# Layer-1 rows and the layer-1 edge sum in one stage of a graph kernel

## The chip, the cores and the metric

The kernel runs on one core of one Trainium2 chip. The metric is the device time of one execution in microseconds (us); lower is better. Engines are named as the profile names them: PE (TensorE matmul) and PEld (its weight loads), DVE (VectorE), ACT (ScalarE), POOL (GpSimd), SP (SyncE); SPq and ACTq are the queues on which SP and ACT issue DMAs.

## What is computed

Two layers over N = 6250 nodes with D = 256 features and E = 200000 edges, of which the second layer matters here:

```python
xn = _layernorm(x, axis=-1)
x = x + _L1_gnn_ref(xn, edge_weight, L1_gnn_W, L1_gnn_b, src, dst)
      + _L1_mix_ref(xn[None], L1_mix_Wq, ..., L1_mix_b2)[0]

def _L1_gnn_ref(x, edge_val, W, b, edge_row, edge_col):
    support = jnp.matmul(x, W)
    gathered = support[edge_col] * edge_val[:, None]
    return jax.ops.segment_sum(gathered, edge_row, num_segments=x.shape[0]) + b

def _L1_mix_ref(x, Wq, Wk, Wv, Wm, W1, W2, g1, b1, g2, b2):
    # Q, K = elu(x Wq)+1, elu(x Wk)+1; KV and sum K over all rows, per head
    msg = _layernorm((Q KV / (Q sum K)) @ Wm, g1, b1)
    h = relu(concatenate([x, msg]) @ W1) @ W2
    return x + _layernorm(h, g2, b2)
```

The first summand is the edge sum: for every edge a row of 256 values is fetched, scaled, and added into the row of another node. The second is row-wise work, once the sums over all rows exist.

## The kernel before

The rows of `x` live in SBUF as 50 blocks of 125 rows (`X[125, 50, 256]`), and row-wise work goes in 25 chunks (NC) of two blocks. Edges have been sorted by target block into records of three words (target, source, weight) in DRAM, and a group is 512 records (SUB = 4 times 128 partitions); there are NG = 391 groups. As a block's edges need not end with a group, the sum goes in NS = 440 steps, each one pair of (group, block). Tables in SBUF say for each step its group (`step_grp`) and block (`step_blk`), and for each group its first step (`first_step`).

**Stages.** `second_layer` does, in one block of straight-line code per engine, an FFN over the 25 chunks (L1148, L1158 on PE, L1484 on DVE), a pass over the chunks for K, V and the table `table1 = xn @ W` (L1189 on PE, L1318 to L1331 on ACT, L1512 on DVE), and then the **rows stage**: 27 turns (`for t in range(NC + 2)`, L1203 on), a software pipeline over chunks. Beside the first two, POOL moves the records into sorted order by indirect DMAs to DRAM (L557, batches of 17) as the positions become known. Then `end_phase()` closes the phase, and `edge_sums` runs as a phase of its own.

**One turn of the rows on PE** (in this order): the product with Wq (L1209), the turned rows of the last message and of `u` (L605), the product with W1 in four parts of which ACT takes pairs with a relu (L1234, ACT L1369), the message matmul (L1242, into two PSUM banks that DVE reads at L635 to L639), the turn of the next rows (L605), the product with Wm (L1255, into bank 6), and the product with W2 (L1264). DVE does the second half of Q (L1536), the last layer norm with its add to `X` (L578 to L592, L1542 to L1551), the division (L635 to L639), and the inner layer norm (L578 to L592, L1531).

**The edge sum.** `edge_walk` gives three parts. SP loads the records of a group (6 KB, L1797) into a ring of RING = 8 slots and, LAG = 4 groups later, waits for that group's gathers and counts `arrived`. POOL waits for the records, reads `first_step`, waits until the steps of the group eight before are `used` (L1820), and issues four indirect DMAs (L1824), each of 128 rows of 1 KB from `table1` into one slot of a ring that lies in `XN`. ACT loads the records of every step once more for DVE. For each step DVE makes the 0/weight matrix (L2142 and four times L2144, `weights`), PE multiplies it with the four gathered tiles into one of two banks (L2128, eight MATMUL records per step) and counts `used`, and DVE adds the bank to the block of `X` (L2156). PE and ACT run loops over 8 steps, DVE runs the first and last 8 steps in straight-line code and the rest in such a loop. Layer 0 has a walk of the same form (`edge_softmax`, loops too) over the same 391 groups and 440 steps, with more matmuls per step.

## Time and profile before

| | us |
|---|---|
| median of three runs | 9435.45 |
| the three runs | 9424.73 to 9456.72 |
| the profiled execution | 9495.87 |
| its span, first to last instruction | 9494.2 |
| PE / DVE / ACT / POOL busy | 5320.2 / 3713.0 / 1980.9 / 4700.6 |
| mean granted TensorE clock, of full speed | 0.763 |

No engine is busy all the time: stages follow each other, and each has a limit of its own. Read by stretches of the profiled execution: head and layer-0 rows up to about 1594, the layer-0 edge walk to about 4340, FFN and K/V of layer 1 to about 6212, the rows stage from there to 6674, the layer-1 edge sum to 9033, and the end (norm, experts, output). POOL's DMA instructions are counted busy while they issue; "idle before" tells how long the engine stood before an instruction and what ended that, where "issue" and "remote" are times in which the profile shows no releaser.

### The profile page before, as it was taken

To read this page: it belongs to the slowest core of one execution; us is meant where nothing else is said; L and a number is where in the kernel's file an instruction comes from. 1 tells how busy PE (TensorE), PEld (TensorE's weight loads), DVE (VectorE), ACT (ScalarE), POOL (GpSimd) and SP (SyncE) were. 2 spreads that over 40 slices of the span, in tenths; PEclk is the share of its full clock that TensorE was granted. 3 is DMA by queue.
4 is the path that set the end of the run, shared out by engine and by line. 5 is a ranking of instruction groups with operands and counts; after the bars stand their busy time and mean duration, and the time that the engine had idled before them with its cause. 6 is when DMAs were issued, how large, how long until landed. Compare 5 with 4: busy or idle time off the path is not lost. (4 is left out here: it accounts for less than half of the span.)

```text
span 9494.2 us, 116847 instructions
## 1 busy us (share of the span) xinstructions
PE 5320.2 (56%) x22050; PEld 3899.7 (41%) x22051; DVE 3713.0 (39%) x14367; ACT 1980.9 (21%) x4706; POOL 4700.6 (50%) x5589
## 2 busy tenths in 40 slices
PE   0431276777877778886053461089444544454469
PEld 0320154455555555554043350078333333333357
DVE  6340154444444444556142240046333333333355
ACT  6110043333333333333021120033000000000034
POOL 3476501555555555554725326600566666666600
PEclk9765577888888888887576685599677777777789
DMA  2100001333333333332000000000233333333300
GB/s 76 30 4 3 5 1 27 86 84 85 84 84 80 78 80 79 81 79 73 3 1 3 2 19 5 5 7 1 76 89 90 89 90 90 91 90 89 89 21 18
DMA packets 505060, 495.26 MB, mean 52 GB/s; under 512 B 374732, under 2 KB 401877, under 8 KB 504149
## 3 DMA queue, kind: packets, MB, share of 16 engines
q0 software_dynamic: 200192, 432.72, 16.7%
q1 hardware_dynamic: 154712, 33.52, 2.0%
q10 hardware_dynamic: 150013, 27.32, 1.7%
q8 instruction: 65, 1.06, 0.0%
q14 instruction: 78, 0.64, 0.0%
HBM read 462.90 MB, written 30.23 MB: 52 GB/s over the span
## 5 line engine op out<-in xcount | busy, mean ns | idle before, releaser
L1824 POOL DMA_INDIRECT XN<-table,XN x3128 | 2988.6, 955 | 993.3 <-issue 935.8
L557 POOL DMA_INDIRECT records<-slot_rec,slot_pos x1564 | 1535.6, 982 | 594.1 <-issue 594.1
L2128 PE MATMUL gcn_psE<-XN,gcn_pE 128*125 x3520 | 1130.5, 485 | 1227.8 <-DVE gcn_pE L2144 905.5
L75 POOL TENSOR_TENSOR cell<-cell 1x1 int32<-1x1 int32 x874 | 162.1, 186 | 2727.2 <-DMA XN<-records 972.7
L2128 PEld LDWEIGHTS gcn_psE<-XN,gcn_pE 128*125 128x125 f32 x3520 | 829.7, 245 | 1528.6 <-issue 1367.3
L1953 PE MATMUL gat_psE<-XN,gat_pE 128*125 x3520 | 1066.1, 455 | 252.7 <-issue 173.1
L1953 PEld LDWEIGHTS gat_psE<-XN,gat_pE 128*125 128x125 f32 x3520 | 751.7, 225 | 399.3 <-issue 275.8
L2156 DVE TENSOR_TENSOR X<-X,gcn_psE 125x256 f32 x440 | 184.4, 419 | 1560.1 <-remote 1113.7
L1937 PE MATMUL gat_psS<-XN,gat_kTs 25*125 25x512 f32 x880 | 586.8, 750 | 152.1 <-ACT XN L1982 113.6
L2144 DVE TENSOR_SCALAR gcn_pE<-iota_n,gcn_lk,gcn_rec 128x125 f32<-128x125 f32 x1760 | 500.7, 364 | 16.0
L1573 ACT ACT_TABLE_LOAD x1 | 1.3, 1283 | 2364.9 <-PEq L117 2364.9
L1944 PE MATMUL gat_psP<-ident,XN 125*128 125x125 f32 x1760 | 309.8, 305 | 198.9 <-ACT gat_sc L2002 148.1
L2032 DVE TENSOR_SCALAR gat_pen<-gat_psB,iota_p 125x512 f32<-125x512 bf16 x440 | 328.7, 747 | 199.6 <-remote 185.0
L2006 ACT ACTIVATE gat_pE<-gat_psP 128x500 f32<-128x500 f32 x440 | 256.9, 584 | 683.4 <-PE gat_psP L1944 349.2
L1944 PEld LDWEIGHTS gat_psP<-ident,XN 125*128 125x128 f32 x1760 | 248.0, 161 | 289.8 <-ACT gat_sc L2002 170.2
L1926 PEld LDWEIGHTS gat_psA<-ident,XN 128*25 128x25 f32 x1760 | 162.6, 113 | 447.8 <-issue 399.2
L1926 PE MATMUL gat_psA<-ident,XN 128*25 128x128 f32 x1760 | 316.4, 310 | 29.2 <-ACT XN L1991 24.3
L1158 PE MATMUL b_bank<-room,b_wf 128*128 128x250 f32 x800 | 193.5, 396 | 246.6 <-issue 161.4
L2043 DVE COPY gat_mo<-edge_m 125x1 f32 x440 | 67.8, 154 | 658.7 <-PE gat_psS L1937 278.1
L1189 PE MATMUL b_bank<-b_wkv,room 128*125 128x256 f32 x400 | 108.9, 433 | 385.3 <-issue 382.1
L745 PE MATMUL a_bank<-room 128*125 128x256 f32 x200 | 74.3, 535 | 432.8 <-ACT room L866 290.1
L2001 ACT ACTIVATE XN<-XN,gat_nm 125x512 f32<-125x512 f32 x440 | 310.9, 707 | 10.2 <-issue 10.2
(448 smaller groups left out, 8516.5 us busy)
## 6 DMA issues: line engine op xcount, KB each, us to landing
XN<-table,XN POOLq DMA_INDIRECT x3128
records<-slot_rec,slot_pos POOLq DMA_INDIRECT x1564
XN<-records SPq DMA_DIRECT2D x782, 6.0 KB
gat_rec<-records ACTq DMA_DIRECT2D x440, 6.0 KB
gcn_rec<-records ACTq DMA_DIRECT2D x440, 6.0 KB
table<-XN ACTq DMA_DIRECT2D x5, 1250.0 KB
table<-room ACTq DMA_DIRECT2D x25, 250.0 KB
out_x<-X SPq DMA_DIRECT2D x25, 250.0 KB
```

Of the source, the lines that this page charges most:

```text
L557: pool.indirect_dma_start(out=rec_d[1], out_offset=bass.IndirectOffsetOnAxis(ap=slot_pos[:, h, j:j + 1], axis=0), in_=slot_rec[:, h, j, :] ...
L1158: last = pe.matmul(psH[i % 2][:, 0:TOK], wf1[:, j, i * P:(i + 1) * P], xT[:, j, :], start=(j == 0), stop=(j == KF - 1))
L1824: pool.indirect_dma_start(out=rows_t[:, s, j, :], out_offset=None, in_=table, in_offset=bass.IndirectOffsetOnAxis(ap=rec_g[:, s, j, 1:2].b ...
L1926: pe.transpose(psA[0:SMALL, j * P:(j + 1) * P], q_rows[:, s % 2, j * SMALL:(j + 1) * SMALL], ident[:, :])
L1937: pe.matmul(psS[d][0:B, :], kTs[:, d, :], qT[:, d, :], start=True, stop=True).then_inc(s_mm, 1)
L1944: last = pe.transpose(psP[:, j * B:(j + 1) * B], pT[:, d, j * P:(j + 1) * P], ident[0:B, 0:B])
L1953: last = pe.matmul(psE[d][0:B, 0:D], pE[:, d, j * B:(j + 1) * B], rows_t[:, slot_of(g), j, 0:D].rearrange("p a w -> p (a w)"), start=(j == ...
L2001: act.activation(pT[:, d, :], S[:, d, :], ACT.Exp, bias=nm[:, d:d + 1], scale=SC, accum_out=rs[:, d:d + 1])
L2006: act.activation(pE[:, d, :], psP[:, 0:SUB * B], ACT.Copy).then_inc(p_done, 1)
L2032: dve.tensor_scalar(pen[:, d, :], psB[0:B, :], iota_p[0:B, 0:1], -BIG, ALU.not_equal, ALU.mult).then_inc(pen_done, 1)
L2128: last = pe.matmul(psE[d][0:B, 0:D], pE[:, d, j, :], rows_t[:, slot_of(g), j, :].rearrange("p a w -> p (a w)"), start=(j == 0), stop=(j == ...
L2144: last = dve.tensor_scalar(pE[:, d, j, :], iota_n[:, :], lk[:, d, j:j + 1], rec_t[:, s, j, 2:3], ALU.is_equal, ALU.mult)
```

## The change

The phase `edge_sums` is gone; its steps are done inside the rows stage of `second_layer`, and what is left of them in a loop at that stage's end.

- **ROWS_ALONE = 12.** Turns 0 to 11 have no steps. In each of the turns 12 to 26 there are four bursts of BURST = 2 steps: 15 x 8 = 120 steps. The other 320 follow in a loop of two steps per iteration.
- **Gathers.** POOL begins them when `rows_free` is set, before turn 0, in a ring `b_ring` of its own (8 slots of 4 KB per partition), since `XN` still holds rows. POOL now waits only for a group's records. It is SP that waits for `used` of the group eight before, and then loads the records into a ring in which DVE also reads them. ACT issues no record loads any more.
- **PSUM.** The steps take banks 6 and 7. Wm's product goes to bank 2 and W1's to banks 4 and 3, which the message matmul also uses, so PE has new waits: the message matmul for ACT's second relu pair (`r_done`) and for `m_done`, Wm's product for DVE's division (`u_done`).
- **Memory and loads.** The FFN's and K/V's weights lie in `b_ring` and are overwritten by the gathers; the other five weights lie in `room` and are loaded after `freed`, beside `src`.
- DVE solves the inner layer norm in the turn of its moments, not at the start of the next.

The core of the diff, in the order SP, POOL, PE (a step, then places of a turn, then the loop), DVE (a burst):

```diff
+ROWS_ALONE = 12
...
+                        def body(t, s):
+                            if not (isinstance(t, int) and t == 0):
+                                n = sp.value_load(first_step[1][0:1, bass.ds((t - 1) * RING + s + 1, 1)], min_val=1, max_val=NS)
+                                sp.wait_ge(used, n)
+                            sp.dma_start(rec_g[:, s, :, :].rearrange("p s w -> p (s w)"),
+                                         rec_v[bass.ds(t * RING + s, 1), :, :].rearrange("g p w -> (g p) w")).then_inc(records[s], 16)
+                            if near(t, s, -LAG):
+                                arrive(*near(t, s, -LAG))
...
                         mv.pool(pool)
+                        pool.wait_ge(mv.settled, 2 * turns)
...
+                        pool.wait_ge(rows_free, 1)
+
+                        def body(t, s):
+                            pool.wait_ge(records[s], t * 16 + 16)
+                            settle(pool, cell[0:1, 0:1], settled, t * RING + s)
+                            for j in range(SUB):
+                                pool.indirect_dma_start(out=ring[:, s, j, :], out_offset=None, in_=table1,
+                                                        in_offset=bass.IndirectOffsetOnAxis(ap=rec_g[:, s, j, 1:2].bitcast(I32), axis=0)).then_inc(got[s], 16)
...
+                        def edge_sum(x, d):
+                            g = group_of(pe, x)
+                            pe.wait_ge(weighed, x + 1)
+                            if not (isinstance(x, int) and x < 2):
+                                pe.wait_ge(added, x - 1)
+                            for j in range(SUB):
+                                last = pe.matmul(psE[d][0:B, 0:D], pE[:, d, j, :],
+                                                 ring[:, bass.ds(g % RING, 1), j, :].rearrange("p a w -> p (a w)"),
+                                                 start=(j == 0), stop=(j == SUB - 1))
+                            last.then_inc(used, 1)
...
+                                    if pair:
+                                        pe.wait_ge(u_done, min(t, NC))
...
+                                if t >= ROWS_ALONE:
+                                    burst()
                             if t < NC:
                                 pe.wait_ge(q_done, t + 1)
                                 pe.wait_ge(u_done, t)
+                                if t >= 2:
+                                    pe.wait_ge(m_done, t - 1)
+                                    pe.wait_ge(r_done, 2 * (t - 2) + 2)
...
                                 pe.wait_ge(m_done, k)
+                                if t < NC:
+                                    pe.wait_ge(u_done, t + 1)
...
+                        with loop(pe, (NS - early_steps) // BURST) as t:
+                            for d in range(BURST):
+                                edge_sum(t * BURST + (early_steps + d), d)
...
+                        def burst():
+                            nonlocal summed
+                            for d in range(BURST):
+                                add_sum(summed + d, d)
+                            summed += BURST
+                            for d in range(BURST):
+                                weights(summed + d, d)
...
-        def edge_sums():
```

In a turn from 12 on, PE's bursts stand behind the first and the second pair of W1, behind the turned next rows and behind Wm's product; DVE's stand behind the second half of Q, behind the last norm with its add, behind the division, and behind the inner norm.

On PE, in one turn of the rows stage before (L1234 is W1's product, the turn begins with L1209):

```order
L1209 MATMUL b_bank<-room 128x250 x4
L605 MATMUL b_bank<-ident,room 128x125 x8
L1234 MATMUL b_bank<-room 128x250 x16
L1242 MATMUL b_bank<-b_kvd,room 125x132 x4
L605 MATMUL b_bank<-ident,XN 128x125 x4
L1255 MATMUL b_bank<-b_wm,room 125x256 x4
L1264 MATMUL b_bank<-b_wm,room 125x256 x8
```

And in the changed kernel in a turn from 12 on, from the turned rows (L606) over the first pair of W1 (L1338) into the first step of the first burst (L1151 reads the group, L1288 is the step's product):

```order
L606 MATMUL b_bank<-ident,room 128x125 x8
L1338 MATMUL b_bank<-room 128x250 x8
L1151 TENSOR_LOAD step_grp
L1151 ISA x2
L1288 ISA
L1288 MATMUL b_bank<-b_ring,room 125x256
L1288 ISA
L1288 MATMUL b_bank<-b_ring,room 125x256
L1288 ISA
L1288 MATMUL b_bank<-b_ring,room 125x256
L1288 ISA
L1288 MATMUL b_bank<-b_ring,room 125x256
```

W1's sixteen matmuls are split into two pairs of eight, and a burst of two steps stands behind each pair, behind the turned next rows, and behind Wm's product.

On POOL, in the loop of the edge sum before, the wait for `used` (with the load of `first_step`) stands ahead of the four gathers of a group:

```order
L1820 ISA
L1820 TENSOR_LOAD first_step
L1820 ISA x2
L74 REGISTER_ALU
L75 TENSOR_TENSOR cell<-cell 1x1
L1824 DMA XN<-table,XN 128x256 x4
```

In the changed kernel that load and its wait stand on SP, ahead of the load of the records for which POOL waits (`room` is where the records now go):

```order
L1181 TENSOR_LOAD first_step
L1181 ISA x2
L1183 DMA room<-records 128x12
L1181 TENSOR_LOAD first_step
L1181 ISA x2
L1183 DMA room<-records 128x12
```

So a group's slot is freed to SP and reaches POOL only by way of the record load.

## Rows read from the trace of the kernel before

**Rows 1.** PE over one turn of the rows stage: start us, us, line, operation, idle before

```profile
6404.02 6.93 PE L1234 MATMUL b_bank<-room 128*128 128x250 f32 x32
6410.79 1.06 PE L1242 MATMUL b_bank<-b_kvd,room 128*125 128x132 f32 x8
...
6412.12 1.89 PE L1255 MATMUL b_bank<-b_wm,room 128*125 128x256 f32 x8
...
6417.30 1.85 PE L1209 MATMUL b_bank<-room 128*128 128x250 f32 x8
...
6421.05 0.62 PE L605 MATMUL b_bank<-ident,room 125*128 125x125 f32 x4 [1.47 <-ACT room L1356]
6421.50 6.93 PE L1234 MATMUL b_bank<-room 128*128 128x250 f32 x32
```

**Rows 2.** ACT in the same turn: the relu of W1's second pair

```profile
6410.99 0.83 ACT L1369 ACTIVATE room<-b_bank,b_bias 128x250 f32<-128x250 f32 x2 [2.55 <-PE b_bank L1234]
```

**Rows 3.** DVE in the same turn: second half of Q, last add, division

```profile
6403.04 0.68 DVE L1536 SCALAR_TENSOR_TENSOR room<-b_bank,room 128x500 f32<-128x500 f32 x1 [2.76 <-ACT room L1352]
...
6409.51 0.69 DVE L1551 TENSOR_TENSOR X<-X,room 125x512 f32<-125x512 f32 x1
...
6412.45 0.76 DVE L639 TENSOR_TENSOR room<-b_bank,b_z 125x256 f32<-125x256 f32 x2
```

**Rows 4.** Busy us (x instructions) of PE, PEld, DVE, ACT, POOL; clock; DMA share; GB/s

```profile
2300.00:2900.00 600.00, 474.58 (x2032) 313.30 (x2032) 291.88 (x1302) 219.90 (x649) 339.77 (x426) 0.83 0.33 84
5610.00:6170.00 560.00, 70.48 (x251) 55.56 (x249) 4.84 (x7) 19.70 (x34) 392.34 (x428) 0.55 0.04 6
6415.00:6674.00 259.00, 234.82 (x1216) 206.55 (x1214) 160.29 (x661) 78.51 (x157) 0.00 (x0) 1.00 0.00 1
7300.00:7900.00 600.00, 288.99 (x911) 212.46 (x912) 194.25 (x681) 0.00 (x0) 402.72 (x502) 0.73 0.33 90
```

**Rows 5.** Start of the edge sum on POOL, its last add on DVE

```profile
6686.47 0.18 POOL L75 TENSOR_TENSOR cell<-cell 1x1 int32<-1x1 int32 x1 [513.22 <-DMA XN<-records]
...
9032.44 0.42 DVE L2156 TENSOR_TENSOR X<-X,gcn_psE 125x256 f32 x1 [1.31 <-PE gcn_psE L2128]
```

**Rows 6.** Groups by line, 6660 to 9050: xcount, busy us, mean ns, idle before

```profile
L1824 POOL DMA_INDIRECT XN<-table,XN x1564 | 1498.1, 958 | 463.6 <-issue 422.1 <-remote 2.1 <-PE gcn_psE L2128 1.8
...
L2144 DVE TENSOR_SCALAR gcn_pE<-iota_n,gcn_lk,gcn_rec 128x125 f32<-128x125 f32 x1760 | 500.7, 364 | 16.0
L2156 DVE TENSOR_TENSOR X<-X,gcn_psE 125x256 f32 x440 | 184.4, 419 | 1560.1 <-remote 1113.7 <-issue 318.2 <-PE gcn_psE L2128 127.0
```

**Rows 7.** A cycle of the edge sum: POOL, then DVE

```profile
7516.91 0.95 POOL L1824 DMA_INDIRECT XN<-table,XN  x1 [0.30 <-issue]
7520.76 0.18 POOL L75 TENSOR_TENSOR cell<-cell 1x1 int32<-1x1 int32 x1 [2.90 <-remote]
...
7520.63 0.42 DVE L2156 TENSOR_TENSOR X<-X,gcn_psE 125x256 f32 x1 [12.46 <-remote]
...
7544.78 0.42 DVE L2156 TENSOR_TENSOR X<-X,gcn_psE 125x256 f32 x1 [11.13 <-remote]
```

**Rows 8.** PE at the end of the edge sum, POOL done

```profile
9020.10 3.71 PE L2128 MATMUL gcn_psE<-XN,gcn_pE 128*125 x16 [0.53 <-DVE gcn_pE L2144]
```

**Rows 9.** FFN chunks on DVE, two ahead of and two during POOL's moves

```profile
4933.06 0.69 DVE L1484 TENSOR_TENSOR room<-b_bank,b_bf 125x512 f32<-125x512 f32 x1 [2.59 <-PE b_bank L1148]
4947.14 0.69 DVE L1484 TENSOR_TENSOR room<-b_bank,b_bf 125x512 f32<-125x512 f32 x1 [2.69 <-PE b_bank L1148]
...
5167.83 0.69 DVE L1484 TENSOR_TENSOR room<-b_bank,b_bf 125x512 f32<-125x512 f32 x1 [112.31 <-remote]
5358.93 0.69 DVE L1484 TENSOR_TENSOR room<-b_bank,b_bf 125x512 f32<-125x512 f32 x1 [171.53 <-remote]
```

**Rows 10.** DMA queues, 5600 to 6180: packets, MB, share of 16 engines

```profile
q8 instruction: 2, 0.03, 0.0%
```

**Rows 11.** DMA issues of the whole page: count, KB each, median us to landing

```profile
slot_rec<-spill_rec SPq DMA_DIRECT2D x92, 25.5 KB, 1.7
```

**Rows 12.** POOL's gathers in 6700 to 9000: min/median/max ns

```profile
L1824 POOL DMA_INDIRECT XN<-table,XN x1541: 943/949/1072, 6699.5 to 8999.2; - x193
```

More of the change, by code:

```diff
@@ L1248, in _ @@
                                 turn_rows(pe, psT, xn_rows, t + 1).then_inc(turned, 1)
+                            if t >= ROWS_ALONE:
+                                burst()
                             if 1 <= t <= NC:
@@ L1257, in _ @@
                                 last.then_inc(g_mm, 1)
+                            if t >= ROWS_ALONE:
+                                burst()
                             if t >= 2:
@@ new lines, in weights @@
+                        def weights(x, d):
+                            g = group_of(dve, x)
+                            rec = rec_g[:, bass.ds(g % RING, 1), :, :].rearrange("p a s w -> p (a s) w")
+                            dve.wait_ge(arrived, g + 1)
+                            if not (isinstance(x, int) and x < 2):
+                                dve.wait_ge(used, x - 1)
+                            steps(dve.tensor_scalar(lk[:, d, :], rec[:, :, 0], step_node[1][:, bass.ds(x, 1)], None, ALU.subtract))
+                            for j in range(SUB):
+                                last = dve.tensor_scalar(pE[:, d, j, :], iota_n[:, :], lk[:, d, j:j + 1], rec[:, j, 2:3], ALU.is_equal, ALU.mult)
+                            last.then_inc(weighed, 1)
@@ new lines, in add_sum @@
+                        def add_sum(x, d):
+                            b = dve.value_load(step_blk[1][0:1, bass.ds(x, 1)], min_val=0, max_val=NB - 1)
+                            ub = one(X[:, bass.ds(b, 1), :])
+                            dve.wait_ge(used, x + 1)
+                            if not (isinstance(x, int) and x < 1):
+                                dve.wait_ge(added, x)
+                            dve.tensor_tensor(ub, ub, psE[d][0:B, 0:D], ALU.add).then_inc(added, 1)
+                        summed = 0
```

223 lines of the change are left out of this document (120 added, 103 removed).

## Prediction

> **What bounds the kernel now.** I read three views, in this order: the table of busy time by stretch, to see which engine each stage leans on; then the timelines of one turn of the rows and of one cycle of the edge sum; then the waits at the edge sum's start and end.
>
> The rows stage is PE's. PE is busy 234.82 of 259 us at full clock and POOL does nothing at all [rows 4]; a turn takes 6421.50 - 6404.02 = 17.48 us, in which PE idles only 1.47 us, waiting for ACT [rows 1]. Turn 12 begins with Q's product at 6417.3 [rows 1].
>
> The edge sum belongs to POOL and to something that POOL's stream does to the others. It runs from 6686.47 to 9032.86 [rows 5]. A gather costs POOL 0.958 us and 0.27 us (422.1 / 1564) of issue [rows 6], so with the settling instruction (0.18 [rows 5]) a group can't go below about 5.1 us; in 600 us POOL does 502 / 5 = 100.4 groups, 5.98 us each, and PE 911 / 8 = 113.9 steps, 5.27 us each [rows 4]. Neither figure is what PE and DVE need: with POOL done, two steps take 3.71 + 0.53 = 4.24 us, 2.12 us each [rows 8]. The cycle shows where the rest goes. POOL issues without a break up to 7517.86, stands 2.90 us, goes on at 7520.76. DVE had stood 12.46 us and goes on at the same moment, 7520.63, then works until 7544.78 - 11.13 = 7533.65 and stands again [rows 7]. So PE and DVE get about **13 us of free running** after each pause of POOL, and next to nothing until the next pause. That this is POOL's stream and not the edge sum's own chain is seen in the FFN, where nobody waits for POOL: a chunk takes 4947.14 - 4933.06 = 14.08 us, but beside POOL's moves, which never pause, 5358.93 - 5167.83 = 191 us [rows 9]; in the K/V pass beside the moves PE is busy 70 of 560 us [rows 4]. I don't know the mechanism; I use the two lengths.
>
> **The change, part by part.** The stretch that changes runs from 6417.3 (turn 12) to 9032.9, 2615.6 us, plus turns 0 to 11.
>
> *Turns 0 to 11, new waits on PE.* The message matmul now waits for ACT's second relu pair: that ends at 6410.99 + 0.83 = 6411.82 [rows 2], while the matmul began at 6410.79 [rows 1]: +1.1 us. Wm's product waits for DVE's division, which ends at 6413.21, 1.4 us after the message matmul's 6411.85 [rows 1, 3], where it used to begin 0.3 us after it: +1.1 us. The 1.47 us wait for ACT hangs on the work behind Wm's product, so it stays. Ten turns of 2.2 us: **+22**.
>
> *Turns 0 to 2, POOL fills its ring.* Eight groups are 41 us of stream without a pause; the free running covers 13, so 28 us are starved. These turns wait for latency anyway; I take **+25** (between 5 and 35).
>
> *Turns 12 to 26.* A turn has 8 steps = 7.1 groups, 36 us of POOL's time at 5.1. PE has 234.82 / 14.8 turns = 15.9 us of rows and 8 times 1.9 to 2.0 us of steps [rows 4, 8], 32 us. DVE has 160.29 / 14.8 = 10.8 and 8 times 500.7 / 440 + 0.42 = 1.56, 23 us [rows 4, 6]. They don't run side by side, though. PE's third burst needs the weights of DVE's second burst, and that stands behind the last norm: from 6403.04 to 6410.20, 7.2 us [rows 3]. Walking through one turn with bursts of 4.0 us on PE and 3.8 us on DVE, PE waits some 6 us there, 3 us ahead of the fourth burst, and 1.5 us for ACT as now: about **42 us of free running a turn**. Some turns' worth of it falls in starved time. Steps free slots, and POOL fills them in one go: 15.3 us free (13 and the 2.3 of the next paragraph) free 2.6 groups, 13 us of stream, then a pause of 2.9 + 2.3; 18.4 us in all for 15.3 of work, a turn of 50 us. Without the 2.3, it is 45.5. The layer-0 walk is the nearest whole case: 2032 matmuls at 22 a step are 92 steps of 6.49 us, with PE busy 5.14 us in each [rows 4], a factor of 1.26; on PE's own 32 us and one wait of 6 that gives 48. I take **49 us**, and keep 42 (7.1 groups at POOL's present 5.98) and 60 as ends. Ring full at turn 12: -10. Together 15 x 49 - 10 = **725**.
>
> *The loop of 320 steps.* DVE and PE do per step what they did. What changes is a slot's way: `used` reached POOL directly, now it reaches SP, which issues the record load, whose landing POOL awaits. The nearest load lands in 1.7 us [rows 11]; with SP's own part 2.3 us more at each pause. PE and DVE run free in it, so it isn't lost: 13 us now carry 24.15 / 5.27 = 4.6 steps, 2.84 us each, so 15.3 us are 5.4 steps, 4.8 groups, 24.4 + 5.2 = 29.6 us, 5.5 a step. ACT's 440 small loads go, which can only help. I take **5.45** (5.27 if the latency costs nothing, 5.8 if it adds fully to each group cycle): 320 x 5.45 = **1744**.
>
> Nothing for the loads of weights after `freed`: their first use is behind the FFN, and POOL, not they, sets the K/V pass. What lies between the rows' end, near 6674, and the first gather at 6686.47 [rows 5] is in the 2615.6 and has no successor.
>
> *Sum:* 22 + 25 + 725 + 1744 = 2516 against 2615.6: **-100 us**. The sum is made against the profiled execution (9495.87, span 9494.2), 0.64% above the median of 9435.45; taken off in proportion it is 99, and gives **9336**.
>
> *A rule against the change.* DVE's weights last 1.14 us a step and now also meet the norms [rows 6]; POOL's gathers take 943/949/1072 ns in all the edge sum [rows 12], so what DVE does beside them costs at most 0.12 us. The Trainium skill, "SBUF — State Buffer", section "Who interferes with whom", says that DVE's `tensor_scalar` in a two-port mode and GpSimd exclude each other for the whole instruction. By that rule 8 x 1.14 = 9 us would be added to a turn's POOL time. The rows don't bear it out.
>
> **Rivals.**
>
> *A. POOL alone sets the pace.* 42 us a turn, 5.27 a step, start-up 10: 22 + 10 + 620 + 1686 = 2338, -277: **9160**. For it: in the cycle PE and DVE need 2.12 of 5.27 us, and POOL paused 15% of the time. Against: the layer-0 walk, whose PE need per group is like a turn's, has POOL at 600 / 85.2 = 7.0 us a group [rows 4].
>
> *B. The steps merely add.* A turn costs its 17.5 and 8 x 5.3 = 60 us, as if the rows only ran where POOL stands: 47 + 15 x 60 - 10 + 1700 = 2637, +21; with 5.27 in the loop and no start-up loss 2598, -18. Between them: **9435**, no change that can be told (I take 0.3%, 28 us, as what a measurement tells).
>
> *C. Slower: the rows starve.* The rows' chain crosses PE, ACT and DVE a dozen times a turn, the edge sum's three times a step. If POOL, whose records are loaded ahead, streams four groups and more in a row as now, a cycle of 24 us has 13 free, and 42 us of turn take 42 x 24.15 / 13 = 78 us; half-way to that, 64: 47 + 950 + 1744 = 2741, +125: **9560**. It decides from 56 us a turn on. For it: the 14-fold FFN chunk in straight-line code [rows 9]. Against: POOL can't stream what isn't freed, and a turn frees a group only each 6 us. One doubt about it can be put aside: if straight-line code starved because its instructions couldn't be fetched, turns would suffer and loops not; but in the 580 us of the crawling K/V pass one such queue moved 2 blocks [rows 10]. The Trainium skill, "Runtime: NRT & Kernel Launch", section "Instruction fetch mechanics", has fetch in blocks of 256 instructions over a DMA queue of its own, mostly hidden; this row agrees.
>
> *D. The record load is the new bound.* With SP starved like the others, a slot takes 5 us and more to reach POOL; 5.8 a step and 52 a turn: 47 + 770 + 1856 = 2673, +57: **9492**.
>
> *E. POOL locked out by DVE* (the rule above as a mechanism): 9 us a turn over 15 turns, +135 on the forecast: **9471**.
>
> **How the numbers follow.** Forecast (turn 46 to 53, -160 to -35): 0.42. A and what lies towards it: 0.23. B: 0.12. C: 0.14. D: 0.07. E: 0.02. Likeliest: 9336. The range must hold 8 in 10: down it takes in A with its 9160, up D and the near side of C: **9160 to 9510**. Faster by over 0.3%: the forecast and A, 0.65. Within 0.3%: B, 0.12. Slower by over 0.3%: C, D, E, 0.23.
>
> **What would show it.** Turns 2 to 11 at 19.7 us from one W1 product to the next, with PE waiting for ACT ahead of the message matmul and for DVE ahead of Wm's. POOL issuing 32 gathers from before turn 0 and then standing until turn 12. Turns from 12 at 46 to 53 us (42: A; 60: B; above 56: C); in the loop 5.3 to 5.6 us a step, with pauses of POOL of some 5 us ended by a record load where they were 2.9. The forecast is wrong if a turn's free-running need isn't near 42 us, or if POOL's short pauses between single groups already let the others run (then A), or don't (then C).

## The result: slower by 1.2%, where 1.1% faster was forecast

| | before | after |
|---|---|---|
| median, us | 9432.50 (4 runs) | 9551.83 (4 runs) |
| lowest to highest | 9424.73 to 9456.72 | 9536.08 to 9578.22 |
| profiled execution, its span | 9495.87, 9494.2 | 9536.08, 9534.4 |
| ratio after / before, 95% interval | | 1.0124, 1.0108 to 1.0139 |

The forecast was 9336 with a range of 9160 to 9510; the time is 216 us above the one and 42 above the other. The two profiled executions differ by only 40 us, since that of before is 63 us above its median and that of after 16 us below. On which chip the first ran isn't on record. A later profile of the same kernel, called before2 below, took 9431.92 us (span 9430.2), and I compare after with that one. Its first message matmul of the rows begins at 6175.5, that of after at 6181.8; what lies behind the last add is 461.4 and 463.6 us. Nearly all of the 104 us between the two spans is in the middle: 2793.3 us in before2, 2889.0 in after.

### The profile after

PE in the turns that have no steps (start, us, engine, line, operation, idle before and what ended it):

```profile
6254.84 1.14 PE L1350 MATMUL b_bank<-b_kvd,room 128*125 128x132 f32 x8 [1.01 <-ACT room L1487]
6257.53 1.96 PE L1367 MATMUL b_bank<-room 128*125 128x256 f32 x8 [1.13 <-DVE room L640]
6274.93 1.14 PE L1350 MATMUL b_bank<-b_kvd,room 128*125 128x132 f32 x8 [1.01 <-ACT room L1487]
```

The two new waits are where the prediction put them, and a turn takes 6274.93 - 6254.84 = 20.09 us where it took 17.48 [rows 1].

A turn with eight steps, in parts: POOL's first operation of a group (L76; its gathers, which follow, are left out), PE, ACT and DVE, from four timelines of the same turn.

```profile
6732.52 0.18 POOL L76 TENSOR_TENSOR cell<-cell 1x1 int32<-1x1 int32 x1 [3.03 <-DMA room<-records]
...
6739.21 0.18 POOL L76 TENSOR_TENSOR cell<-cell 1x1 int32<-1x1 int32 x1 [1.26 <-DMA room<-records]
...
6744.72 0.22 POOL L76 TENSOR_TENSOR cell<-cell 1x1 int32<-1x1 int32 x1
...
6748.97 1.85 PE L1310 MATMUL b_bank<-room 128*128 128x250 f32 x8
...
6749.82 0.19 POOL L76 TENSOR_TENSOR cell<-cell 1x1 int32<-1x1 int32 x1
...
6754.89 0.18 POOL L76 TENSOR_TENSOR cell<-cell 1x1 int32<-1x1 int32 x1
6755.67 0.23 DVE L1651 TENSOR_SCALAR room<-room,step_node 128x4 f32 x1 [4.45 <-issue]
...
6762.71 0.59 ACT L1468 ACTIVATE room<-b_bank 128x500 f32<-128x500 f32 x1 [14.60 <-DMA X<-in_x]
...
6764.56 1.07 PE L606 MATMUL b_bank<-ident,room 125*128 125x125 f32 x4 [13.31 <-ACT room L1474]
...
6773.75 0.18 POOL L76 TENSOR_TENSOR cell<-cell 1x1 int32<-1x1 int32 x1 [13.81 <-DMA room<-records]
```

From 6739.21 POOL streams four groups without a pause. PE's product with Wq, which ACT needs, is over at 6750.82 by the profile (the ends of matmuls are modelled), but ACT starts on it at 6762.71, when the stream is over (the DMA named there was long done). PE stands 13.31 us, and then it is POOL that waits for 13.81 us, since nobody had freed a slot. Over the last eleven pitches (from the start of one message matmul to the start of the next) a turn takes 55.5 us.

The trace also has the times of the semaphore updates, and they say what was late. The update that tells ACT of the product is recorded at 6762.69, 11.87 us behind the product's end, and ACT starts 0.02 us later. In the turns without steps from turn 2 on it comes 0.01 us behind the end. In ten of the twelve turns 13 to 24 it comes 4.7 to 13.0 us behind it, each time 1.9 to 3.0 us after the end of POOL's last gather. So ACT was ready, and it is PE's signal (or the true end of the matmul, which the profile doesn't show) that came late. PE's waits for ACT at this place in the turns with steps (us in total, times, longest):

```profile
PE b_bank L606 <- ACT room L1474: 123.4, 13, 14.5
```

That is 9.5 us a turn where it was 1.47 [rows 1].

The loop. Busy us by stretch of the last 320 steps (PE, PEld, DVE, ACT, POOL, clock, DMA share, GB/s), first of before2, then of after:

```profile
7314.00:8969.00 1655.00, 814.24 (x2553) 599.24 (x2551) 545.06 (x1910) 0.00 (x0) 1109.45 (x1384) 0.73 0.33 90
```

```profile
7266.00:9070.00 1804.00, 806.92 (x2542) 578.97 (x2543) 583.63 (x1908) 0.00 (x0) 1102.00 (x1374) 0.73 0.29 81
```

PE's and POOL's work is the same; the stretch takes 149 us longer. Where they went is seen in what POOL's settling operation, the first of each group, waited for in these stretches (us in total, times, longest). Before2:

```profile
POOL cell L75 <- remote: 173.4, 69, 3.3
POOL cell L75 <- PE gcn_psE L2128: 12.7, 11, 2.4
POOL cell L75 <- issue: 8.7, 16, 0.8
```

After:

```profile
POOL cell L76 <- DMA room<-records: 333.8, 92, 11.9
POOL cell L76 <- issue: 17.1, 15, 2.2
```

That is 194.8 against 350.9 us. The loop is POOL's stream plus POOL's pauses. Between the starts of the first and the last of the 320 adds it is 1654.5 - 194.8 = 1460 us in before2, 1805.3 - 350.9 = 1454 in after. This sum is used in all that follows. It came out at 1440 to 1470 us for every kernel on such chips with whole gathers and the settling operation unchanged, whatever was done to the steps.

### The profile page after: what moved, and what is told of

It reads as the page before. It is cut to its first block and busy times, and to the rows that moved or that the text cites. A ratio compares the mean times of both kernels' runs of the same rounds, so it can differ in the third digit from the quotient of the medians.

```text
span 9534.4 us, 117269 instructions
## 1 busy us (share of the span) xinstructions
PE 5231.6 (55%) x22050; PEld 3839.0 (40%) x22051; DVE 3769.7 (40%) x14367; ACT 1979.1 (21%) x4706; POOL 4696.8 (49%) x5590
## 5 line engine op out<-in xcount | busy, mean ns | idle before, releaser
L1992 POOL DMA_INDIRECT XN<-table,XN x1564 | 1486.5, 950 | 528.3 <-issue 511.9
L1205 POOL DMA_INDIRECT b_ring<-table,room x1564 | 1497.5, 957 | 469.8 <-issue 432.2
L1288 PE MATMUL b_bank<-b_ring,room 128*125 x3520 | 1071.6, 463 | 1181.7 <-DVE room L1653 803.6
L76 POOL TENSOR_TENSOR cell<-cell 1x1 int32<-1x1 int32 x874 | 166.4, 190 | 2749.4 <-DMA room<-records 810.6
L1288 PEld LDWEIGHTS b_bank<-b_ring,room 128*125 128x125 f32 x3520 | 782.7, 231 | 1462.3 <-issue 1324.0
L2121 PE MATMUL gat_psE<-XN,gat_pE 128*125 x3520 | 1040.9, 446 | 253.1 <-issue 175.2
L1653 DVE TENSOR_SCALAR room<-iota_n,room 128x125 f32<-128x125 f32 x1760 | 515.0, 355 | 272.3 <-issue 195.8
L1662 DVE TENSOR_TENSOR X<-X,b_bank 125x256 f32 x440 | 185.4, 421 | 742.1 <-issue 339.9
L1651 DVE TENSOR_SCALAR room<-room,step_node 128x4 f32 x440 | 107.1, 243 | 595.4 <-issue 449.9
L1240 PE MATMUL b_bank<-room,b_ring 128*128 128x250 f32 x800 | 192.4, 396 | 242.3 <-issue 236.8
L1271 PE MATMUL b_bank<-b_ring,room 128*125 128x256 f32 x400 | 111.9, 442 | 374.7 <-issue 369.9
```

The source lines that it names most:

```text
L1205: pool.indirect_dma_start(out=ring[:, s, j, :], out_offset=None, in_=table1, in_offset=bass.IndirectOffsetOnAxis(ap=rec_g[:, s, j, 1:2].bi ...
L1288: last = pe.matmul(psE[d][0:B, 0:D], pE[:, d, j, :], ring[:, bass.ds(g % RING, 1), j, :].rearrange("p a w -> p (a w)"), start=(j == 0), st ...
L1653: last = dve.tensor_scalar(pE[:, d, j, :], iota_n[:, :], lk[:, d, j:j + 1], rec[:, j, 2:3], ALU.is_equal, ALU.mult)
L1992: pool.indirect_dma_start(out=rows_t[:, s, j, :], out_offset=None, in_=table, in_offset=bass.IndirectOffsetOnAxis(ap=rec_g[:, s, j, 1:2].b ...
L2121: last = pe.matmul(psE[d][0:B, 0:D], pE[:, d, j * B:(j + 1) * B], rows_t[:, slot_of(g), j, 0:D].rearrange("p a w -> p (a w)"), start=(j == ...
```

## The experiments

Two theories on the loop, each from a line of the change, and one on the turns:

- **F**, VectorE's step got longer. It is three things in one: a register load of the group, register addresses for the records, and the wait for the group's gathers (`arrived`), which TensorE had before. With POOL done, an add, its 0.68 us gap and the weights take 2.98 us a step where they took 2.12 [rows 8]:

```profile
9057.11 0.42 DVE L1662 TENSOR_TENSOR X<-X,b_bank 125x256 f32 x1 [0.57 <-issue]
...
9059.92 0.42 DVE L1662 TENSOR_TENSOR X<-X,b_bank 125x256 f32 x1 [0.21 <-issue]
9061.02 0.23 DVE L1651 TENSOR_SCALAR room<-room,step_node 128x4 f32 x1 [0.68 <-issue]
9061.40 1.11 DVE L1653 TENSOR_SCALAR room<-iota_n,room 128x125 f32<-128x125 f32 x4
9063.08 0.42 DVE L1662 TENSOR_TENSOR X<-X,b_bank 125x256 f32 x1 [0.57 <-issue]
```

Two steps take 9063.08 - 9057.11 = 5.97 us.

- **D**, the record load stands between a freed slot and POOL (rival D of the prediction).
- **C**, in the turns the rows starve beside POOL's stream (rival C).

A group of runs shares one chip, and each ratio is against before on that chip. "Turn" is the mean of the last eleven pitches; "loop" is us a step over the last 320 steps (from the first to the last of their adds, divided by 319); "waits" is what POOL's settling operation waited there, in us. A chip "starves" where the other engines nearly stop beside POOL's stream, as in rows 9.

| kernel | chip's before | ratio (95%) | turn | loop | waits |
|---|---|---|---|---|---|
| before2 | 9436.6 | one run | 17.5 | 5.19 | 195 |
| after | 9432.5 | 1.0124 (1.0108 to 1.0139) | 55.5 | 5.66 | 351 |
| f_before | 9434.5 | 1.0224 (1.0182 to 1.0265) | 17.5 | 5.62 | 326 |
| d_before | 9434.5 | 1.0101 (1.0081 to 1.0121) | 17.5 | 5.43 | 289 |
| own_records | 9434.5 | 1.0092 (1.0063 to 1.0121) | 58.3 | 5.38 | 275 |
| pool_waits | 9434.5 | 0.9994 (0.9982 to 1.0007) | 53.5 | 5.40 | 266 |
| hoist_after | 9514.7 | 1.0132 (1.0111 to 1.0152) | 56.1 | 5.82 | 395 |
| hoist_pool | 9514.7 | 0.9969 (0.9959 to 0.9978) | 51.3 | 5.48 | 294 |
| both_undone | 9514.7 | 0.9934 (0.9918 to 0.9951) | 54.8 | 5.23 | 215 |
| alone_26 | 9514.7 | 1.0284 (1.0267 to 1.0301) | 20.1 | 5.67 | 339 |
| pace_d | 9505.6 | 1.0025 (1.0010 to 1.0041) | 54.4 | 5.54 | 218 |
| early_own2 | 9505.6 | 0.9869 (0.9840 to 0.9898) | 54.6 | | |
| quarter | 6736.3 | one run | 42.6 | 2.98 | |
| pace_a | 6736.3 | 1.0326 (1.0309 to 1.0343) | | 4.85 | |
| pace_b | 6736.3 | 1.1072 (1.1054 to 1.1091) | | 6.13 | |
| after2 | 6723.5 | 1.0085 (1.0068 to 1.0102) | 42.6 | 4.44 | 1 |
| pace_c | 6723.5 | 1.0323 (1.0306 to 1.0341) | 44.6 | 4.86 | |
| early_pool | 6723.5 | 1.0118 (1.0101 to 1.0135) | 41.0 | | |
| early_own | 6723.5 | 1.0378 (1.0361 to 1.0395) | 47.8 | | |

### f_before and d_before: each suspect alone, in the kernel before

f_before gives VectorE the form of a step that it has in the changed kernel (the records lie in 16 slots, addressed by the group, and ScalarE loads them there). The wait for `arrived` goes from PE to DVE with it:

```diff
 def weights(t, s):
     x, d = t * RING + s, s % 2
+    g = group_of(dve, x)
+    rec = rec_t[:, bass.ds(g % 2 * RING + s, 1), :, :].rearrange("p a s w -> p (a s) w")
+    dve.wait_ge(arrived, g + 1)
     dve.wait_ge(rec_ready[s], t * 16 + 16)
```

d_before moves the wait for `used`:

```diff
 # SyncE
+    if which and not (isinstance(t, int) and t == 0):
+        n = sp.value_load(first_step[which][...])
+        sp.wait_ge(used, n)
     load_records(sp, t * RING + s, rec_g[:, s, :, :], group_ready[s])
```

> The kernel before, with only VectorE's part of a step written as in the changed kernel: the group is read from its table into a register, the wait for the gathers stands on VectorE, and the five reads of the records go by a register. GpSimd and SyncE are untouched. Theory F (VectorE's step got longer: 2.98 us instead of 2.12 with GpSimd done, so fewer steps fit into a cycle of free running): slower, by 0.1 to 0.4 us a step, 9480 to 9600 against 9433. Theory D (the record load in a slot's way back to GpSimd): no change, within 20 us of 9433.

> The kernel before, with only the wait for `used` of the second walk moved from GpSimd to SyncE, ahead of the record load. VectorE's step is untouched. Theory D: each of the 80 odd pauses of GpSimd gets about 1 to 2.3 us longer and ends in a record load, 5.45 to 5.8 us a step in place of 5.23: 9510 to 9680. Theory F: within 30 us of 9433.

Measured: 9636.39 and 9533.85 us against 9434.54, so +202 and +99. Both theories hold, and each alone is dear; F's price is above the 47 to 167 us that were expected. The two don't add up: the loops lose 0.43 and 0.24 us a step, the changed kernel with both loses 0.47. POOL's waits in the last 320 steps tell how. F:

```profile
POOL cell L75 <- PE gcn_psE L2131: 243.1, 67, 9.8
POOL cell L75 <- remote: 74.8, 42, 2.9
```

D:

```profile
POOL cell L75 <- DMA XN<-records: 274.0, 67, 5.4
POOL cell L75 <- issue: 15.3, 11, 2.2
```

Counting pauses of over 1 us in that stretch: before2 has 75 of 2.46 us on average, F 96 of 3.24, D 70 of 3.99, and after, with both, 90 of 3.73. In the changed kernel with only F left (pool_waits, below) it is 99 of 2.56, with only D left (own_records) 68 of 3.86. **F makes more pauses, D makes each longer**; in f_before they also got longer. With F fewer steps, so fewer freed slots, fit between two pauses (3.3 in place of 4.3), and that is what I had left out.

No run takes the three parts of F from each other. What the moved wait ended is on record, though:

```profile
DVE gcn_lk L2148 <- SPq L1804: 41.0, 16, 6.7
```

In before2 PE waited 3.5 us for the same count in these 320 steps. The moved wait is a part of F, then, and the instructions need not be all of the rest. What F adds with POOL done is seen at this kernel's end, where each step has a gap that before does not have:

```profile
9162.14 0.42 DVE L2162 TENSOR_TENSOR X<-X,gcn_psE 125x256 f32 x1
9163.18 0.23 DVE L2148 TENSOR_SCALAR gcn_lk<-gcn_rec,step_node 128x4 f32 x1 [0.62 <-issue]
9163.55 1.11 DVE L2150 TENSOR_SCALAR gcn_pE<-iota_n,gcn_lk,gcn_rec 128x125 f32<-128x125 f32 x4
9164.79 0.42 DVE L2162 TENSOR_TENSOR X<-X,gcn_psE 125x256 f32 x1
```

A step is 9164.79 - 9162.14 = 2.65 us here, 0.53 more than the 2.12 of before. Over 440 steps the 202 us are 0.46 each, so F costs about what it adds to a step with POOL done. In that gap stand one register load, 0.31 us by the trace, and five short instructions that the profile doesn't count as busy either. The Trainium skill, "Runtime: NRT & Kernel Launch", section "Instruction fetch mechanics", gives about 200 ns for a register load. The trace has half as much again for the load alone.

### own_records and pool_waits: each suspect taken out of the changed kernel

own_records: ScalarE loads the records of every step once more, 8 at a time in a turn, into 16 slots with fixed addresses; VectorE reads those.

```diff
+    if t >= ROWS_ALONE:                       # ScalarE, in a turn
+        first = 8 * (t - ROWS_ALONE)
+        for x in range(first + 8 if first else 0, first + 16):
+            step_records(x, x)
...
 def weights(x, d, ...):                       # VectorE
-    g = group_of(dve, x)
-    rec = rec_g[:, bass.ds(g % RING, 1), :, :]...
-    dve.wait_ge(arrived, g + 1)
+    rec = rec_t[:, base % SLOTS, :, :]
+    dve.wait_ge(rec_ready[base % SLOTS], ...)
```

pool_waits: 16 record slots, SyncE loads ahead, POOL waits for `used` as before the change.

```diff
 # SyncE
-    sp.wait_ge(used, n)
-    sp.dma_start(rec_g[:, s, ...], ...)
+    sp.dma_start(rec_g[:, h * RING + s, ...], ...)
 # POOL
     pool.wait_ge(records[h * RING + s], ...)
+    n = pool.value_load(first_step[1][...])
+    pool.wait_ge(used, n)
```

> The changed kernel, with VectorE's records loaded once more for each step by ScalarE into a ring of 16 slots with fixed addresses (the wait for the gathers is TensorE's again, the loop of VectorE has 16 steps an iteration). SyncE's wait and record load stay. Theory F: VectorE's step back to 2.1 us free; 5.35 us a step in the loop instead of 5.66 and turns of 50 us instead of 55.4: about 9370. Theory D: within 40 us of 9552. Theory C (the rows starve in the turns, whatever a step costs): the loop gains, about 100 us, the turns stay at 54 us or more: about 9450.

> The changed kernel, with the wait for `used` on GpSimd as before the change, and the records of a group loaded ahead by SyncE into a ring of 16 slots. VectorE's step stays as long as it is. Theory D: pauses go from 3.7 us back to 2.7, some 100 us in the loop and the like share in the turns: 9400 to 9450. Theory F: less than 60 us, 9500 to 9550. Theory C: turns stay at 54 us or more in either case.

Measured: 9515.92 and 9428.12. In the loop both give back what was expected (5.66 to 5.38 and to 5.40; waits 351 to 275 and to 266), the one as much as the other, though F had been twice as dear as D in the kernel before. In the turns they part: pool_waits brings 55.5 down to 53.5, own_records takes it up to 58.3, so that its total misses F's 9370 and C's 9450 and lies where D alone would have put it. The turns rise most likely because ScalarE's eight loads stand in the middle of the rows' chain (early_own and early_pool, below, differ in the same way; no run isolates the loads). So theory C survives in both: with either suspect out, a turn stays above 53 us.

pool_waits equals before within its interval: the overlap gains what F and the starved turns cost.

### hoist_after, hoist_pool, both_undone, alone_26

The hoist moves VectorE's load of the group ahead of the wait for `used`, where four weight instructions are still in work:

```diff
 def add_sum(x, d, ahead=False):
     b = dve.value_load(step_blk[1][0:1, bass.ds(x, 1)], ...)
+    g = group_of(dve, x + BURST) if ahead else None
     dve.wait_ge(used, x + 1)
```

> The changed kernel, with one instruction moved on VectorE: a step's register load of its group stands ahead of the wait for `used`, beside that of the block, where four weight instructions of the step before are still in work. Theory F by exposure (what hurts is that the load of 0.68 us stands behind the wait): nearly all that VectorE's form cost comes back, 5.4 us a step in the loop instead of 5.66, 9552 - 90 or more: 9400 to 9470. Theory F by count (each instruction costs in starved time, wherever it stands): under 30 us, 9520 to 9560.

> The same with the wait for `used` on GpSimd and the records loaded ahead into 16 slots. Theories F (exposure) and D together: 5.2 us a step in the loop, turns of 50: 9428 - 70 to - 110, so 9320 to 9360, under both kernels. F by count: 9400 to 9430.

> The changed kernel with VectorE's records loaded by ScalarE for each step and the wait for `used` on GpSimd, so both parts of a step as before the change: the loop has to run at the 5.2 to 5.25 us of before (F and D are all that there is), 320 x 0.42 = 135 less than 9552. The turns: 58 us as in the kernel with ScalarE's loads alone if it is these loads that hold up the rows, 50 if it was not. 9400 with the first, 9300 with the second.

> The changed kernel with ROWS_ALONE = 26: 8 steps in the last turn, 432 in the loop. If a turn of 55.4 us is one of 20.1 plus 8 steps of 4.4 us, the overlap gives 1.25 us for each of the 112 steps moved, and undoing it costs 140: 9690. Theory C (the rows starve so much that a step in a turn costs what it does in the loop): 9552 within 30.

hoist_after: ratio 1.0132, no better than the 1.0124 of after, with 395 us of waits in the loop. **Theory F by exposure fell**: it matters little on which side of the wait the load stands. Its end, with POOL done, shows why the hoist could bring nothing:

```profile
9165.48 0.42 DVE L1663 TENSOR_TENSOR X<-X,b_bank 125x256 f32 x1 [0.92 <-issue]
9165.88 0.23 DVE L1651 TENSOR_SCALAR room<-room,step_node 128x4 f32 x1
...
9168.65 0.42 DVE L1663 TENSOR_TENSOR X<-X,b_bank 125x256 f32 x1 [1.28 <-issue]
...
9171.45 0.42 DVE L1663 TENSOR_TENSOR X<-X,b_bank 125x256 f32 x1 [0.92 <-issue]
```

The gap behind the add is gone, and the gap ahead of it has grown from 0.21 and 0.57 us to 0.92 and 1.28. Two steps take 9171.45 - 9165.48 = 5.97 us, what they took in after. The load was moved, not hidden. So these runs speak for F by the length or the number of the instructions, which they can't tell apart. hoist_pool gained 0.25% on pool_waits (0.9969 against 0.9994, on two chips), in its turns (51.3 us), not in its loop.

both_undone: the loop is back at 5.23 us a step and its waits at 215 us, so F and D together are all of the loop's loss. At 0.9934 it is faster than both kernels, though its turns of 54.8 us lie between the 58 and the 50 that were expected.

alone_26 is the same code with the overlap undone. It cost 1.0284 / 1.0124, 1.6% or 150 us, with 140 expected: a step in a turn does cost (55.5 - 20.1) / 8 = 4.4 us, one in the loop 5.7. **The overlap works**; it is bought with a dearer step and a dearer slot.

### quarter: what a turn needs

One of a group's four gathers is issued, on top of pool_waits; it leaves out the other three, so three quarters of the gathered rows are stale:

```diff
-    for j in range(SUB):
+    for j in range(SUB if isinstance(t, int) and t == 0 else 1):
         pool.indirect_dma_start(out=ring[:, s, j, :], ...)
```

> The kernel with the wait for `used` on GpSimd and 16 record slots, in which GpSimd fetches only one of a group's four tiles (the first eight groups are fetched whole), so three quarters of the gathered data are stale: a group costs GpSimd 1.5 us and its stream is never long. It shows what a turn and a step need when nobody is starved. Theory C (in a turn, what lies above the forecast's 42 us of free running is starvation by GpSimd's stream): turns of 40 to 44 us, steps of 3.0 us in the loop, 8450 to 8550. Rival (the turn's chain is simply longer than it was walked through): turns of 50 us and more, 8600 and up.

Message matmuls of two turns in a row, and VectorE's adds of the loop:

```profile
4742.29 1.06 PE L1365 MATMUL b_bank<-b_kvd,room 128*125 128x132 f32 x8
4784.73 1.06 PE L1365 MATMUL b_bank<-b_kvd,room 128*125 128x132 f32 x8
```

```profile
5835.91 0.42 DVE L1677 TENSOR_TENSOR X<-X,b_bank 125x256 f32 x1 [0.57 <-issue]
...
5841.88 0.42 DVE L1677 TENSOR_TENSOR X<-X,b_bank 125x256 f32 x1 [0.58 <-issue]
```

42.44 us a turn (42.6 over eleven) and 2.98 us a step. The walk had said 42. This run came onto a chip where POOL's stream starves nobody (next section), and there the changed kernel with all its gathers (after2) takes 42.6 us a turn too. So it is the pair after and after2, one kernel on two chips, that gives the price: 55.5 - 42.6 = 12.9 us a turn beside POOL's stream. Of these, 8 are in the wait shown above. On after2 the same wait is

```profile
PE b_bank L606 <- ACT room L1474: 18.3, 13, 1.5
```

and PE's update for ACT comes 0.01 us behind the product's end in every turn. The granted clock was lower in the turns of after as well, 0.81 against 0.89, but PE's busy time there is 508 against 485 us for the 15 turns, which is 1.5 us a turn. The rest is then C's, not the rows' own chain.

### after2, pace_a, pace_b, pace_c, early_pool, early_own: chips that don't starve

The chip of quarter ran before in 6736 us, and another one in 6723, where the others need 9430 to 9520. The kernels are the same. What differs is the thing that I had taken for a property of the kernel. FFN chunks beside POOL's moves, on after2:

```profile
3271.50 0.69 DVE L1602 TENSOR_TENSOR room<-b_bank,b_bf 125x512 f32<-125x512 f32 x1 [2.31 <-PE b_bank L1230]
3285.58 0.69 DVE L1602 TENSOR_TENSOR room<-b_bank,b_bf 125x512 f32<-125x512 f32 x1 [2.53 <-PE b_bank L1230]
```

14.08 us, where before took 191 beside the same moves [rows 9]. On these two chips POOL's stream starves nobody, and every stage with such a stream is short.

> The changed kernel unchanged. On a chip that starves: ratio 1.012 again. On a chip without starvation: a turn is 42.5 us or a little more, its 7.1 groups taking 36 us of GpSimd; a step in the loop is bound by GpSimd, 5.07 x 391 / 440 = 4.5 us, before and after alike; per step moved a turn saves 4.5 - (42.5 - 20.1) / 8 = 1.7 us, 120 of them 204, less 2.6 x 12 = 31 for the new waits: ratio 0.975.

After2 shows the expected turn (42.6 us) and loop (4.44 us a step, POOL alone; it waits 0.8 us in 320 steps), and yet the ratio is 1.0085, not 0.975. One row points at the reason. PE, the first step of turn 12:

```profile
4251.61 3.77 PE L1288 MATMUL b_bank<-b_ring,room 128*125 x8 [322.53 <-DVE room L1653]
```

PE stood 322.53 us. Turn 0 begins near 3700 us here, and 27 turns of 17.5 us would end near 4172, ahead of POOL's moves (4238 us). So the kernel before has its whole rows stage beside the moves, where it costs nothing. The changed kernel keeps 15 turns back to mix them with steps, and steps can't begin before the records are in place. It then pays in POOL's time: 58.0 us of waits for records in the turns,

```profile
POOL cell L76 <- DMA room<-records: 58.0, 18, 6.5
```

which matches the 57 us of the result (6780.27 - 6723.47). That before hides all 27 turns there is worked out from these rows and not shown; before2, meant to show it, came onto a chip that starves. The time that its expectation works out for such a chip, 6712 us, is 11 us under the 6723 measured on the chip of after2.

> The kernel before, unchanged. On a chip without starvation (near 6730): the K/V pass and all 27 turns of the rows end before GpSimd's moves do, near 4240, so the rows cost nothing there, and the edge sum takes 440 x 4.5 = 1980 us bound by GpSimd; 4240 + 30 + 1980 + 462 = 6712. Rival: some turns stand behind the moves, 17.5 us each, and the edge sum is quicker than GpSimd's 5.07 us a group allow, which can't be. On a chip that starves: turn 0 near 6180 to 6250, pauses of GpSimd of about 200 us in the last 320 steps, 9430 to 9520.

It showed there what the section on the result uses: 9431.92 us, turn 0 near 6175, 195 us of waits.

On the other kernels these chips say little of starvation, and the expectations for it came to nothing:

> The same kernel, whole, with GpSimd's tiny settling operation ahead of each group's gathers made larger (125x256 in place of 1x1, an estimated 0.3 to 0.6 us a group). Theory P (short gaps in GpSimd's stream feed the others as well as its long pauses do): cycles vanish, turns go from 54 to 47 or less, the loop to 5.1 to 5.3 us a step; 9428 - 100 to - 150. Rival (only a real standstill frees them, any work on GpSimd just adds): 391 groups of 0.4 us, some + 100: 9530.

> The same with three such operations in a row, an estimated 1 to 1.8 us a group. Theory P: no starvation is left, the turn is the larger of 42 us and 7.1 groups of 6.5 us = 46, the loop 5.8 us a step by GpSimd alone: 9400 to 9450. Rival: + 400 us or more.

> The kernel with the wait for `used` on GpSimd and 16 record slots, with the settling operation of 125x256 (0.62 us instead of 0.18) ahead of each group's gathers; the same kernel as pace_a, to be seen on a chip on which GpSimd's stream starves the others (before near 9430 to 9520). There theory P (short gaps feed the others): turns of 47 us or less, ratio to before 0.97 to 0.985. Rival (a gap of half a us feeds nobody): 391 x 0.45 = 175 us more, ratio 1.01 to 1.02. On a chip without starvation (before near 6736) it repeats 1.033.

> The kernel with the wait for `used` on GpSimd, 16 record slots and the group's register load ahead of the wait, with ROWS_ALONE = 2: 80 more steps in turns. A step in a turn costs 4.0 to 4.2 us, one in the loop 5.4: 80 x 1.2 = 96 us less than with 12: ratio to before 0.985 to 0.99 on a chip that starves. Theory C (early turns starve more, since GpSimd starts with an empty ring): 0.995 or more.

> The kernel with both parts of a step as before the change (ScalarE's record loads for VectorE, `used` on GpSimd), with ROWS_ALONE = 2. 80 steps move from 5.2 to 4.2 us: ratio 0.985 on a chip that starves, in place of 0.9934 with 12.

The larger settling operation took 0.62 us, as in this row of pace_d,

```profile
7704.37 0.63 POOL L1220 TENSOR_TENSOR b_wr<-b_wr 125x256 f32<-125x256 f32 x1
```

and where POOL is the only bound, work on it merely adds: pace_a and pace_c lie 3.3 and 3.2% above before, pace_b, with three of them, 10.7%. early_pool shows turns of 41.0 us and early_own of 47.8, the difference being, most likely, ScalarE's eight loads a turn; with more turns held back from under the moves both are slower than after2.

### pace_d and early_own2: the same two on a chip that starves

pace_d, on top of pool_waits:

```diff
-    settle(pool, cell[0:1, 0:1], settled, t * RING + s)
+    for i in range(1):
+        pool.wait_ge(settled, (t * RING + s) * 1 + i)
+        pool.tensor_tensor(wr[:, :], wr[:, :], wr[:, :], ALU.subtract).then_inc(settled, 1)
```

early_own2 is both_undone with ROWS_ALONE = 2.

> The same kernel as pace_a and pace_c, once more for a chip that starves. Theory P (short gaps feed the others): turns of 47 us or less, ratio to before 0.97 to 0.985. Rival (a gap of half a us feeds nobody): 391 x 0.45 = 175 us more than the 9428 of its base, ratio 1.01 to 1.02. On a chip without starvation it repeats 1.032.

> The same kernel as early_own, once more for a chip that starves: 80 steps more in turns, each 1.0 us cheaper there than in the loop: ratio 0.985, in place of 0.9934 with ROWS_ALONE = 12. Rival: ScalarE's 8 loads a turn hold up the rows as in early_own (47.7 us a turn instead of 42.5 without starvation), and starvation comes on top: turns of 58 and more, ratio 1.00.

pace_d: 1.0025, between the two theories. POOL's operations got 391 x 0.44 = 172 us longer, the kernel only about 30 (0.9994 to 1.0025). In the loop the stream took 92 us more by the sum of the first section (1768 - 218 = 1550 against 1723 - 266 = 1457), and the waits fell by 48; the turns stayed at 54.4. So a gap of half a us doesn't pay for itself. Whether it feeds the others a little, or the waits are only shorter because POOL comes to them later, isn't told apart.

early_own2: 9391.24 against 9505.62, **ratio 0.9869**, as expected. It beats before here, and after by its ratio of 1.0124: 80 more steps went into turns of 54.6 us, and the second layer's steps have their short form. On a chip that doesn't starve the same kernel is 3.8% slower than before (early_own). Which of the two is better is a question of the chip, not of the code.

## Why the prediction was wrong, by its own steps

| term | predicted | measured | |
|---|---|---|---|
| turns 0 to 11, new waits and start | +47 | 242.0 - 194.5 = +47.5 (after, before2) | right |
| free need of a turn | 42 | 42.6 (quarter) | right |
| turns 12 to 26 | 725 (49 a turn) | 836 (55.5) | +111 |
| loop of 320 steps | 1744 (5.45) | 1811 (5.66) | +67 |
| record load, per step in the loop | +0.18 | +0.24 (5.19 to 5.43, d_before) | near |

*Turns 0 to 11.* These are measured from the message matmul of turn 0 to Q's product of turn 12. From the message matmul of turn 0 to that of turn 2 it takes 53.0 us instead of 30.6 in before2, 22 for the filling of the ring where 25 were said; a turn is 2.6 us longer where 2.2 were said. That the sum is met to half a us is luck: the two misses cancel.

*Turns 12 to 26.* The mechanism was right, the size of one term was not: the starved time. The free need of 42 us wasn't luck. On after2 PE waits 136 us for DVE's weights in these turns (458.8 without the 322.5 ahead of turn 12), 9.1 a turn, where the walk had 6 and 3. I let POOL stream 2.6 groups at a time with a pause behind each, and got 7 us of starved time a turn. The turn shown above has four groups in one go, all turns have 3.0 between two pauses on average, not far above the 2.6, and yet the price is 12.9 us. What I got wrong is whom the stream meets. The free 42 us are not spread evenly over the turn: a turn's steps free slots in bunches, and in the middle, where PE waits for ACT through Q, nothing is freed at all, so POOL first runs out its stream while nobody works and then stands for records (13.8 us in the turn shown). PE's signal to ACT there came 4.7 to 13.0 us late in ten of twelve turns. A mean rate hides that. Rival C named it, with 56 us a turn as the point from which it decides and 64 as its price; 55.5 is just short of that point.

*The loop.* The step that failed is the sentence "DVE and PE do per step what they did". PE does, but for the wait for `arrived`, which went to VectorE. VectorE's part went from one register load and static addresses to two loads and an address instruction ahead of every read of the records; the order of the changed kernel shows it, and I had read it for PE, SP and POOL alone. f_before puts this line at 202 us in the kernel before, twice the record load's 99, and the record load was the only thing I priced. In the changed kernel the two are worth about the same, 0.28 and 0.26 us a step (own_records, pool_waits).

*The rest.* 111 + 67 = 178 of the 216 us. Another 16 are that the profiled execution of after lies below its own median, and 17 that the stretch in the profiled execution of before was longer than in before2 (2810 against 2793).

*Rivals.* The time is that which C gave (9560), but not by C alone: C's turns came a little short and the loop went over half of the way to D's 5.8 us a step, through F as much as through the record load. F was not on my list; with F taken out (own_records, D left in) it is at 5.38, a little under the 5.45 forecast. A is out by the turn shown above: POOL had 13.8 us to spare. E, VectorE locking POOL out, found nothing again: on after2 VectorE is as busy as ever and POOL's 320 steps take 1415 us, all stream.

## What to carry over

When two stages are laid over each other, count the instructions of the moved step on every engine, those that a profile doesn't count as busy too; a register load, register addresses and a wait that moved onto the engine in the middle of the chain cost 0.46 us a step in the kernel before, about what they add to a free step, and twice an extra DMA in a slot's way; out of the changed kernel both were worth the same. Moving a load helps only if the step gets shorter by it: look at that first. Where loop time is one engine's stream plus its pauses, write it so: the number of pauses and the length of one answer to different causes, and each experiment then shows which it changed. And look at what the moved stage was hidden behind where it stood: on two of the chips the rows were, as far as can be worked out, free before the change.

## What the runs showed of the hardware

- The same program took 9430 to 9520 us on some chips and 6723 to 6736 on two others, with no difference in the code. On the first, VectorE, ScalarE and TensorE all but stop beside a stream of GpSimd's indirect DMAs without pauses (FFN chunk 191 us [rows 9], busy 4.84, 19.70 and 70.48 of 560 us [rows 4]); on the others they don't (14.08 us). GpSimd's part of a gather lasts the same, 946 ns (median) in before2 and 947 in after2. The runs don't say what differs between the chips. Among the first, too, one chip is 0.85% above another (9514.7 and 9434.5).
- On the first kind a semaphore update of TensorE was recorded up to 13.0 us behind the modelled end of its matmul, 1.9 to 3.0 us after GpSimd's last gather had ended, and ScalarE started 0.02 us after the update (after, turns 13 to 24). On after2's chip the same update came 0.01 us behind in all 25 turns. Whether the update or the matmul's true end is late, the trace doesn't show.
- In before the others ran free for about 13 us from a pause of 2.90 us on [rows 7]. With a settling operation longer by 0.44 us at each group, POOL's waits in the loop were 218 us where they had been 266, on another chip, and the turns no shorter: such gaps give back less than they cost.
- A register load on VectorE takes 0.30 us (median, before2 and after). Behind a wait, with the short instructions around it, it leaves a gap of 0.6 to 0.7 us. Ahead of the wait it lengthens the gap there by as much: two steps take 5.97 us either way with POOL done. Beside POOL's stream the hoist brought nothing in the loop (5.82 us a step, against 5.67 of alone_26 on that chip).
